# Attention exponentials of units 2 to 6 computed from tanh on their own, and the router exponentials of seven units at once behind the last tanh

## What is computed

```
h   = tanh(txt_proj[t] + feat_proj[token] + b)          # 4096 tokens x 77 rows x 256 features
rho = h @ w  (+ mask);   att = softmax(rho) over the 77 rows
w_s = tanh(att @ ctx @ Wcw + bcw);  b_s = tanh(att @ ctx @ Wcb + bcb)
x   = x + w_s * layernorm(x) + b_s
y   = layernorm(x)
probs = softmax(y @ gate) over 8 experts                 # the router
each expert: its top 512 of 4096 tokens by probs -> gelu FFN, scaled by probs, added back
shared FFN: gelu(y @ Ws1 + bs1) @ Ws2 + bs2, added for every token
```

## Time and profile before

| | |
|---|---|
| Median of 3 runs | 893.89 us (893.71 to 893.97) |
| Span of the profiled execution, first to last instruction | 892.1 us |
| PE busy, PEld busy | 801.3 us (90%), 472.7 us (53%) |
| ACT busy | 767.8 us (86%) |
| DVE busy | 708.7 us (79%) |
| POOL busy | 307.6 us (34%) |
| Chain that ended last, by engine | PE 39%, ACT 38%, issue 11%, DVE 9%, POOL 1% |

### The profile page before, as it was taken

How to read it: one execution, slowest core, us unless ns; L and a number is a source line. 1 busy time by engine, 2 the same in 40 slices (tenths; PEclk the granted TensorE clock), 3 DMA queues, 4 the chain that set the end, 5 groups by cost and what they waited for, 6 DMA issues and landing times.

```text
span 892.1 us, 14125 instructions
## 1 busy us (share of the span) xinstructions
PE 801.3 (90%) x5385; PEld 472.7 (53%) x5385; DVE 708.7 (79%) x1405; ACT 767.8 (86%) x601; POOL 307.6 (34%) x537
## 2 busy tenths in 40 slices
PE   7975679569998999999999999999988999999996
PEld 5321123124443444445454455545766899999986
DVE  5899889898989689988878995894887877676641
ACT  3989999999999999999999999997753677676672
POOL 3310540615543007674002740052203145555424
PEclk9899999999999999999999999999999999999998
DMA  8000000000001000200000010002202365544513
GB/s 267 19 1 0 1 1 1 1 24 15 10 9 40 1 1 25 71 2 1 24 1 1 25 48 1 24 1 89 77 24 78 98 181 142 136 106 132 137 20 41
DMA packets 32406, 41.82 MB, mean 47 GB/s; under 512 B 2365, under 2 KB 29011, under 8 KB 32339
## 3 DMA queue, kind: packets, MB, share of 16 engines
q1 hardware_dynamic: 26083, 32.49, 10.9%
q0 software_dynamic: 6144, 8.39, 5.7%
q10 hardware_dynamic: 112, 0.04, 0.0%
HBM read 28.33 MB, written 12.58 MB: 46 GB/s over the span
## 4 chain that ended last, share of the span: by engine, by line
PE 39%; ACT 38%; issue 11%; DVE 9%; POOL 1%; DMA 0%; POOLq 0%; ACTq 0%; DVEq 0%
ACT z L995 31%; PE bank L914 10%; PE bank L937 9%; PE bank L787 7%; DVE z L1372 4%; PE bank L829 3%; PE bank L844 3%; ACT z L991 2%; ACT u L1038 2%; PE bank L763 2%; PE bank L715 1%; PE bank L952 1%; PE bank L817 1%; ACT L1038 1%; PE bank L888 1%
## 5 line engine op out<-in xcount | busy, mean ns | idle before, releaser
L995 ACT ACTIVATE z<-z 128x4096 f32<-128x4096 f32 (+5 forms) x157 | 520.9, 3364 | 4.6 <-DVE z L1372 4.4
L1372 DVE TENSOR_SCALAR z<-feat,txt_bias 128x1024 f32<-128x1024 f32 (+1 forms) x722 | 421.9, 656 | 36.5 <-PE bank L787 35.6
L787 PE MATMUL bank<-z,window 128*32 128x512 f32 x2464 | 304.9, 604 | 64.0 <-ACT z L995 62.5
L787 PEld LDWEIGHTS bank<-z,window 128*32 128x32 f32 x2464 | 70.0, 110 | 249.7 <-issue 134.1
L844 PE MATMUL bank<-ws_sb,u 128*128 128x256 f32 x512 | 126.3, 387 | 5.6 <-ACT u L1038 5.6
L844 PEld LDWEIGHTS bank<-ws_sb,u 128*128 128x128 f32 x512 | 92.2, 189 | 41.1 <-issue 19.8
L829 PE MATMUL bank<-tr,ws_s 128*128 128x512 f32 x384 | 107.9, 417 | 0.0
L914 PE MATMUL bank<-xg_s,w_s 128*128 128x512 f32 x384 | 99.5, 397 | 0.2 <-DVE xg_s L1672 0.2
L937 PEld LDWEIGHTS bank<-w_s,hid_s 128*128 128x128 f32 x672 | 86.3, 188 | 4.0
L937 PE MATMUL bank<-w_s,hid_s 128*128 128x256 f32 x672 | 88.2, 280 | 0.0
L1074 ACT ACTIVATE hid<-bank,vec 128x512 f32<-128x512 f32 x64 | 44.2, 690 | 49.3 <-PE bank L914 49.2
(11 more groups left out here) (264 smaller groups left out, 750.4 us busy)
## 6 DMA issues: line engine op xcount, KB each, us to landing
w_raw<-in_L_ffn_W_dram SPq DMA_DIRECT2D x16, 1024.0 KB, 5.6
x_ring<-in_x_dram SPq DMA_DIRECT2D x8, 512.0 KB, 7.9
xn_dram<-xn SPq DMA_DIRECT2D x8, 512.0 KB, 2.9
out_dram<-x_ring SPq DMA_DIRECT2D x8, 512.0 KB, 3.2
u<-in_L_ffn_Ws_dram SPq DMA_DIRECT2D x1, 1024.0 KB, 11.0
ws_sb<-in_L_ffn_Ws_dram SPq DMA_DIRECT2D x1, 1024.0 KB, 13.7
xg<-xn_dram,idx POOLq DMA_INDIRECT x32, 4.1
out_dram<-y,idx POOLq DMA_INDIRECT x32, 3.9
```

Of the source, the lines that this page charges most:

```text
L787: ins = e.matmul(sums[v][32 * r:32 * r + 32, :], window[:, c, 31 - k:63 - k], z[:, n % ZB, at_piece:at_piece + TOK], start=(v, r) not in b ...
L995: e.activation(part, part, ACT.Tanh).then_inc(signal(*step), 1)
L1372: ins = e.tensor_scalar(z[:, n % ZB, i * width:(i + 1) * width], feat_of(units, c), bias_of(units, t, c), None, ALU.add)
```

## The change

The attention exponential of units 2 to 6 is no longer an exp. ACT computes tanh(-x/2) in its place, and a new DVE step `exp_close` of three instructions makes exp(x) = 2 / (1 + tanh(-x/2)) - 1 of it: add 1, reciprocal, times 2 minus 1, each 128 x 320 and each waiting for the one before. Units 0, 1 and 7 keep the exp. The tail tables get one more place, for `exp_close`; in `TAIL_EARLY` the exponential also moves from place 4 to 2 and `weigh` from 5 to 4, in `TAIL_SINGLE` `weigh` moves from 3 to 4 and `gates` from 5 to 6.

The router exponentials of units 0 to 6 become one ACTIVATE of 128 x 224 behind the last tanh (`early_exp`), their sums and reciprocals one pair of DVE instructions (`early_sums`), and product and shift another pair (`early_probs`), which stands behind `att_shift` of unit 7. POOL's `values` becomes one step over all 32 tiles at the end.

```diff
-TAIL_EARLY = (0, 0, 1, 4, 5, 5, 5, 4, 11, 6, 10, 12, 12, 14)
+TAIL_EARLY = (0, 0, 1, 2, 3, 4, 4, 5, 4, 11, 6, 10, 12, 12, 14)
...
-        return [[("rho_out", v)], [("rho_turn", v)], [("att_shift", v)], [("att_exp", v)], [("weigh", v)],
+        return [[("rho_out", v)], [("rho_turn", v)], [("att_shift", v)], [("att_exp", v)],
+                [("exp_close", v)] if UPB <= v < vb else [], [("weigh", v)],
...
-        for v in ([early - UPB, late - UPB] if bb > 1 else []):
-            at_slots(base, (3, 5), probs_of(v))
...
-    for v in (va - 2, va - 1):
-        at_slots(base, (2, 5), probs_of(v))
-    at_slots(base, (5,), [[("values", 0, NT - 2 * J)]])
...
-    order += [("logits_exp", va), ("router", va), *end[0], *(step for step in lead if step[0] == "up"), *end[1],
-              ("load_w1", 0), ("load_w2", 0), *end[2], ("att_exp", vb)]
+    order += [("early_exp",), ("early_sums",), *end[0], *(step for step in lead if step[0] == "up"), *end[1],
+              ("load_w1", 0), ("load_w2", 0), *end[2], ("att_exp", vb), ("early_probs",)]
...
-                    e.activation(att[:, v % 2], att[:, v % 2], ACT.Exp).then_inc(signal(*step), 1)
+                    if not through_tanh(v):
+                        e.activation(att[:, v % 2], att[:, v % 2], ACT.Exp).then_inc(signal(*step), 1)
+                    else:
+                        e.activation(att[:, v % 2], att[:, v % 2], ACT.Tanh, scale=-0.5).then_inc(signal(*step), 1)
...
+                elif kind == "early_exp":
+                    e.wait_ge(*done("logits_shift", va))
+                    e.activation(lg[:, 0:vb], lg[:, 0:vb], ACT.Exp).then_inc(signal(*step), 1)
...
-                    first, end = args
-                    tiles = slice(first, end)
-                    shape = [P, end - first, E]
-                    if first == 0:
-                        e.wait_ge(consts, CONSTS)
...
+                    shape = [P, NT, E]
+                    e.wait_ge(consts, CONSTS)
...
+                elif kind == "exp_close":
+                    v, = args
+                    a = att[:, v % 2]
+                    e.wait_ge(*done("att_exp", v))
+                    link(e.tensor_scalar(a, a, 1.0, None, ALU.add))
+                    e.wait_ge(vector_link, linked)
+                    link(e.reciprocal(a, a))
+                    e.wait_ge(vector_link, linked)
+                    e.tensor_scalar(a, a, 2.0, -1.0, ALU.mult, ALU.add).then_inc(signal(*step), 1)
...
+                elif kind == "early_sums":
+                    e.wait_ge(*done("early_exp"))
+                    e.wait_ge(*done("split_b2"))
+                    link(e.tensor_reduce(early_total, early_lg, AX.X, ALU.add))
+                    e.wait_ge(vector_link, linked)
+                    e.reciprocal(early_inverse, early_total).then_inc(signal(*step), 1)
+                elif kind == "early_probs":
+                    e.wait_ge(*done("early_sums"))
+                    known = slice(0, vb * J)
+                    link(e.tensor_tensor(probs[:, known, :], early_lg, early_inverse.unsqueeze(2).broadcast_to([P, vb * J, E]), ALU.mult))
+                    e.wait_ge(vector_link, linked)
+                    e.tensor_scalar(bits[:, known, :], probs[:, known, :].bitcast(I32), 31 - 2 * HALF_BITS, None,
+                                    ALU.logical_shift_left).then_inc(signal(*step), 1)
```

More of the change, by code:

```diff
@@ L235, in split @@
         return [("split_hi", name, ex, h), ("split_lo", name, ex, h)]
-    end = tail(vb)
+    end = [steps for steps in tail(vb) if steps]
     end[7] = [("y_scale_last", vb)]
@@ L257, in work_order @@
     held.clear()
-    order += [*end[7], *end[9], *end[8], ("logits_exp", vb), ("y_shift_last", vb), ("router", vb), ("values", NT - 2 * J, NT)]
+    order += [*end[7], *end[9], *end[8], ("logits_exp", vb), ("y_shift_last", vb), ("router", vb), ("values",)]
     order += [step for step in lead if step[0] == "down" and step[1:3] in late]
@@ L470, in xattn_moe_kernel @@
         b2_raw = eq[0:B2_ROWS, :]
+        early_units = UNITS - 1
+        early_lg = lg[:, 0:early_units].rearrange("p v j e -> p (v j) e")
+        early_total, early_inverse = [eq[:, i * NT:i * NT + early_units * J] for i in range(2)]
         b2_s = sb("b2_s", [B2_ROWS, D], F32R)
@@ L551, in up_bank, with through_tanh @@
             return RHO[m] if v == va and m < 2 else UP[m % 2]
+        def through_tanh(v):
+            return UPB <= v < vb
         EMPTIES = {
@@ L1233, in _ @@
                 elif kind == "values":
-                    first, end = args
-                    tiles = slice(first, end)
-                    shape = [P, end - first, E]
-                    if first == 0:
-                        e.wait_ge(consts, CONSTS)
[L1239 to L1242, removed]
+                    shape = [P, NT, E]
+                    e.wait_ge(consts, CONSTS)
+                    e.tensor_copy(vals[:, :, :, 0], tok_tile[:].unsqueeze(2).broadcast_to(shape))
+                    e.tensor_copy(vals[:, :, :, 1], tok_part[:, 0:1].unsqueeze(2).broadcast_to(shape))
+                    e.wait_ge(*done("early_probs"))
+                    e.wait_ge(*done("router", vb))
+                    link(e.tensor_copy(vals[:, :, :, 2], probs[:]))
                     e.wait_ge(pool_link, linked)
-                    link(e.tensor_tensor(rest[:, tiles, :], probs[:, tiles, :], vals[:, tiles, :, 2], ALU.subtract))
+                    link(e.tensor_tensor(rest, probs[:], vals[:, :, :, 2], ALU.subtract))
                     e.wait_ge(pool_link, linked)
-                    link(e.tensor_copy(vals[:, tiles, :, 3], rest[:, tiles, :]))
+                    link(e.tensor_copy(vals[:, :, :, 3], rest))
                     e.wait_ge(pool_link, linked)
-                    e.tensor_tensor(vals[:, tiles, :, 4], rest[:, tiles, :], vals[:, tiles, :, 3],
+                    e.tensor_tensor(vals[:, :, :, 4], rest, vals[:, :, :, 3],
                                     ALU.subtract).then_inc(signal(*step), 1)
@@ L1253, in _ @@
                     if ex == 0:
-                        e.wait_ge(*done("values", NT - 2 * J, NT))
+                        e.wait_ge(*done("values"))
                         e.wait_ge(stored[2], 16)
@@ L1631, in _ @@
                     if ex == 0:
-                        e.wait_ge(*done("values", 0, NT - 2 * J))
-                        e.wait_ge(*done("values", NT - 2 * J, NT))
+                        e.wait_ge(*done("values"))
                     else:
```

10 lines of the change are left out of this document (4 added, 6 removed).

## The result

The changed kernel takes 893.02 us (median of 19 runs, 891.23 to 894.46) beside 893.91 for the kernel before (19 runs in turn with them). The ratio is 0.9985 with a 95% interval of 0.998 to 0.9991: 0.9 us won where 7.0 were predicted. The predicted time and the whole of its range, 884.6 to 890.6 us, are missed.

A forecast was written before the change was run, and what follows sets the result against it. ACT was taken to set the pace while PE had idle time to give up: lead 4.85 + 2.33 = 7.2 us, less 0.2, took the span from 892.1 to 885.1, plus 1.8 gave 886.9 us; range 885.8 to 887.7, widened 884.6 to 890.6.

The forecast's parts named there:

- What DVE gains and loses: DVE over the stage: closing step 1.2 us, 2.1 at the upper end; 6.0 us more, some 4.4 less, in total nothing.
- signs of being wrong: Reciprocal over 1.4 us, ACT waiting for DVE over 2 us, PE idle time not ending with ACT, or counting starting later.
- What ACT loses: ACT ahead of the last tanh: 3 x 2.9 = 8.7 us of work removed, a load costing 1.28 us without a drain.
- First pair: Blocks 83 to 85: ACT waits 0.95 us for DVE's sums, so its lead is 1.95 us, not 2.9.
- Second pair: Blocks 122 to 124: DVE's sums just fit, so 2.9 us are won and ACT's lead becomes 4.85 us.
- Single: Unit 6: DVE not in the way, ACT wins another 2.9 us to a lead of 7.75; 7.2 us reach 618.8.
- PE as the second bound: PE in the stage: the gain is capped by its idle time, 10.6 us in all, 2.33 us of it at the single.
- Behind the last tanh: After the last tanh: added router work hidden by PE and slack, 0.2 us lost beside POOL; 273.3 us to the end as before.
- The first rival: DVE becomes the bound at the pairs, closing step 2.1 us or more: gain 4.5 to 5.5 us, 889 us; chance 0.17.
- The rival for slower: Closing steps over 4.3 us at the pairs cost more than ACT's 2.9 us; at 5 us each 897 us; chance 0.03.

The follow-up runs named there:

- e5: Changed kernel with each closing step cut in two halves, each behind its own block, and weigh and gate_in of a pair's first unit one block later: 893.07 us.
- e3: Changed kernel with the tanh way for unit 6 only, units 2 to 5 keeping exp at its old places, 10 loads: 890.11 us.
- e4: Changed kernel with the router part alone, every attention exponential an exp, 12 loads: 893.05 us.
- e1: Changed kernel with the reciprocal removed from the closing step, so attention weights are not the softmax: 885.71 us.
- e2: Changed kernel with two reciprocals, one behind the other, in each closing step, so attention weights are not the softmax: 907.39 us.
- e6: Changed kernel with tanh at the second pair and the single only, first pair with exp at its old places, 8 loads: 892.34 us.
- e10: Changed kernel with ACT itself adding one of four pieces in 8 blocks, 83 to 86 and 122 to 125: 888.7 us.
- e7: Changed kernel with ACT itself adding one of four pieces in 14 blocks, 83 to 89 and 122 to 128: 886.95 us.
- e9: Kernel before, without the change, with ACT itself adding one of four pieces in blocks 83 to 89 and 122 to 128: 896.46 us.

## Why the prediction was wrong

The step that failed is "What DVE gains and loses", and in it one term: the reciprocal of 320 elements, taken as 0.5 us with 1.4 as its upper end. It took 2.15 us. Three of the prediction's own signs of being wrong are there: a reciprocal over 1.4 us, waits of ACT for DVE over 2 us, and idle time of PE that doesn't end with ACT. The row it rested on is the earlier trace rows, a reciprocal of 4 elements, 14 ns longer than a product. At 4 elements nearly all of 178 ns is the cost of an instruction whatever its size; the price of an element doesn't show there. The changed kernel holds two more sizes: 328 ns at 28 and 2153 at 320 elements. (328 - 178) / 24 and (2153 - 328) / 292 are both 6.25 ns: the three lie on one line, with 6.25 ns for an element and 153 ns beside it. e5's halves of 160 elements lie on it as well, 1.15 us. From the same line 4 elements make 25 ns, but a product's 4 elements are in its 164 ns too, and its fixed part may be another; a difference of 14 ns between two kinds of instruction, each with a fixed part of its own, could bear no slope at all. The Trainium skill (VectorE: DVE Perf Modes, section Walkthrough: the 8-slice pipeline in each mode) gives the reciprocal a repeat count of 8; the estimate that the prediction made from it and set aside, 2.7 us, was nearer than the rows' 0.5. The measured 2153 ns are 6.8 times the 318 ns of the plain instruction of the same width beside it.

The other steps, point by point:

- "What ACT loses", 8.7 us and no drain at a load: right, 8.3 us of busy time are gone and e3 against e4 gives 2.5 to 2.9 us for two loads.
- "First pair": the order and the arithmetic were right, the size was not. It put the end of the sums of block 84 at 329.1 and of block 85 at 334.5. With 1.6 us more for the closing step these are 330.7 and 336.1; the trace has 330.62 and 335.8. The tanh of block 85 starts at 335.87 instead of 336.45 before, a lead of 0.58 instead of 1.95 us. The closing step of the second unit, which the sum put at nothing, takes 0.47 of it, and 0.51 us at the second pair.
- "Second pair": the same. It was to win 2.9 us and "just fit"; the tanh of block 124 starts at 484.95, 0.18 us later than in the earlier trace rows.
- "Single": right. DVE isn't in the way there. ACT wins 2.66 us up to the last tanh in e3 against e4, and 2.46 of them reach DVE's fetch.
- PE as the second bound: right in e1, where 0.81 us of idle time are left from 473 to 574 us. The changed kernel came to it as well, by a path that the prediction doesn't name. DVE works from 471.51 to 540 us without waiting for anything (in e1 from 468.63 to 533), the closing steps of the second pair lie in that stretch, and what DVE writes behind them comes later by their length. One of these is `tr`, which `up` (L828) of PE reads: its last part is written from 511.86 to 512.55 us, and PE has waited 1.91 us for it. From there to its last contraction PE has no idle time left. The rows of PE in the changed kernel and in e1:

```profile
512.65 1.63 PE L828 MATMUL bank<-tr,ws_s 128*128 128x512 f32 x6 [1.91 <-issue]
```

```profile
505.93 1.63 PE L828 MATMUL bank<-tr,ws_s 128*128 128x512 f32 x6 [0.40 <-issue]
```

  The profile names no releaser in these rows, but in the chain that ended last DVE's L1507 stands right ahead of the first of them. The wait is there in the changed kernel and in e2, e5, e6 and e10 (1.9 us each), and not in the kernel before, e3, e4, e7 and e9; in e1 it is 0.40. So the reciprocal costs twice, in ACT's waits for the sums and in PE's wait for `tr`, and here the second decides when the stage ends.
- "Behind the last tanh": right in its length. DVE fetches the sums at 617.18, not at 611.6, and from there to the end are 890.1 - 617.18 = 272.9 us, where 273.3 were forecast. The row beside that of the earlier trace rows:

```profile
617.18 0.69 DVE L1427 COPY rho_sb<-bank 128x512 f32<-128x512 f32 x1 [1.02 <-PE bank L786]
```

- The first rival was the true mechanism, at the wrong size: it named DVE at both pairs and the second unit's step as well, and stopped at a closing step of 2.1 us. It gave 889 us; with 2.8 us the losses go on and eat both pairs. The rival for slower counted with 4.3 us as the point where the pairs turn into a loss against before. e2, at about 5 us a step, shows 907 us, where that rival had 897: it left out that lateness adds up over a pair, the second units' steps and the single.

What stays open: between e1 and the changed kernel the spans differ by 890.1 - 883.9 = 6.2 us, and ACT's waits for the sums by 10.7 - 5.4 = 5.3 by the profile pages' line of the tanh. `up` starts 512.65 - 505.93 = 6.7 us later, and DVE's fetch behind PE's last contraction 617.18 - 611.09 = 6.1, so PE's path accounts for the difference of the spans. No run removes PE's wait for `tr` alone. The other long wait of PE in this stage, 1.90 us for `xn` at 400.12, isn't a piece of the difference: e1 has it too, with 1.69 us, and ACT is busy in all of the 40 us from 400 to 440.

## What to carry to other kernels

A duration read at one small size carries no slope: before an instruction is put into an engine's order at 80 times the size, find two sizes of it, or leave the upper end where the worst reading of its mechanism puts it. Work taken off the engine that sets the pace is worth only what its feeder can follow: count what the exchange puts on the feeder at the place itself, not over the stage, and follow everything that the feeder writes next, here `tr` for PE as well as the sums for ACT. And where an exchange loads the feeder, look for a second exchange the other way: 14 pieces at 0.2 us of ACT's time gave back 4.6 us of span, though alone they cost 2.6.

## What the runs showed of the hardware

The reciprocal's 6.25 ns for an element of a partition: 178 ns at 4 elements, 328 at 28, 1150 at 160 and 2153 at 320.

The early fall of the clock. In the profiles of e3, e4 and e6, PE's granted clock is 0.72 over 34 to 40 us, in all others shown here 1.00. The row of e4 and that of the changed kernel:

```profile
34.00:40.00 6.00, 6.00 (x28) 1.98 (x27) 5.70 (x14) 6.00 (x6) 0.00 (x0) 0.72 0.00 0
```

```profile
34.00:40.00 6.00, 6.00 (x31) 2.50 (x30) 5.71 (x14) 6.00 (x6) 0.00 (x0) 1.00 0.00 0
```

PE in order of time in e4, and then in the changed kernel:

```profile
33.61 1.12 PE L714 MATMUL bank<-ident,xn 128*128 128x128 f32 x8 [1.97 <-POOL xn L1139]
34.66 3.53 PE L786 MATMUL bank<-z,window 128*32 128x512 f32 x16
```

```profile
33.60 1.09 PE L714 MATMUL bank<-ident,xn 128*128 128x128 f32 x8 [1.68 <-POOL xn L1139]
34.62 1.92 PE L786 MATMUL bank<-z,window 128*32 128x512 f32 x16
```

Behind a wait of 1.97 us for POOL the 16 matmuls of a block take 3.53 instead of 1.92 us, as at 1.2 instead of 2.4 GHz, and what follows is some 1.7 us later (ACT's tanh at 317.29 us in the changed kernel starts at 318.96 in e4). The wait alone doesn't decide it: in e2's profile it is 1.97 us as well, and the matmuls behind it take 1.92 us at a granted clock of 1.00. The same is seen later on. In e6 the clock falls behind the wait of 1.92 us for `tr` (six matmuls in 2.61 us), while behind the changed kernel's 1.91 us for `tr` the same six take 1.63. In e10 it falls behind 1.85 us at 398 us, in e2 behind 2.28 us at 496 us and 1.88 at 622. Why it falls in some executions and not in others stays open.
